# Gated retention: one matmul per four heads' exponents, with the split running sums flattened through HBM

## The reference, cut to what matters

```python
q = rmsnorm(x @ Wq); k = rmsnorm(x @ Wk); v = rmsnorm(x @ Wv)
g = x @ Wg
gt = jax.nn.log_sigmoid(x @ Wgt) / 16.0            # one log decay per token and head
...
bc = jnp.cumsum(g, axis=-1)                        # here g is gt, summed inside a chunk
decay = jnp.exp(bc[..., :, None] - bc[..., None, :])
A = jnp.einsum('bhnid,bhnjd->bhnij', q, k) * jnp.where(mask, decay, 0.0)
o_intra = jnp.einsum('bhnij,bhnjd->bhnid', A, v)
...                                                # plus what the chunks before hand on
o = rmsnorm(o)
o = jax.nn.silu(g) * o
return o @ Wo
```

## Time and profile before

| what | value |
|---|---|
| median of 3 runs | 2580.32 us (2579.85 to 2581.23) |
| profiled execution, its own time | 2581.53 us |
| its span, first to last instruction | 2579.4 us |
| busy share of the span | PE 91%, DVE 62%, ACT 43%, POOL 34% |
| mean granted TensorE clock | 0.963 |
| gated retention, first to last exponents of it | 1150.9 to 1998.7 us |

### The profile page before, as it was taken

How to read it: one execution, slowest core, us unless ns; L and a number is a source line. 1 busy time by engine, 2 the same in 40 slices (tenths; PEclk the granted TensorE clock), 3 DMA queues, 4 the chain that set the end, 5 groups by cost and what they waited for, 6 DMA issues and landing times. The chain is left out here.

```text
span 2579.4 us, 55940 instructions
## 1 busy us (share of the span) xinstructions
PE 2337.8 (91%) x20985; PEld 1606.7 (62%) x21080; DVE 1603.8 (62%) x3416; ACT 1102.1 (43%) x2397; POOL 875.9 (34%) x1231
## 2 busy tenths in 40 slices
PE   8988999999999997989999999999998799839996
PEld 6765666666666665556656666666665699726664
DVE  1227787777777776656666666666666499862222
ACT  2333333333333331236666666666665244402221
POOL 1111010111011110015566665666655355532342
PEclk9999999999999998989999999999999799859998
DMA  5100000000000000220000000000000022231330
GB/s 166 41 1 2 1 0 0 0 0 0 0 0 0 0 0 11 75 65 1 0 0 0 0 0 0 0 0 0 0 0 1 1 71 92 75 103 50 125 104 29
DMA packets 52744, 65.20 MB, mean 25 GB/s; under 512 B 5970, under 2 KB 45607, under 8 KB 52697
## 3 DMA queue, kind: packets, MB, share of 16 engines
q1 hardware_dynamic: 49624, 56.47, 6.8%
q0 software_dynamic: 3072, 8.07, 1.0%
HBM read 43.88 MB, written 20.97 MB: 25 GB/s over the span
## 5 line engine op out<-in xcount | busy, mean ns | idle before, releaser
L369 PE MATMUL B_ps_s<-B_xk,B_xT 128*32 128x308 f32 x4096 | 284.9, 424 | 12.8 <-ACT B_xk L504 12.8
L390 PE MATMUL B_ps_m<-B_wo,B_oT 128*128 128x256 f32 x1024 | 239.5, 387 | 2.1 <-ACT B_oT L523 2.1
L1513 DVE TENSOR_TENSOR D_att<-D_ps_s,D_dexp 128x1024 f32<-128x1024 f32 x128 | 154.5, 1207 | 131.9 <-ACT D_dexp L1331 122.4
L1083 POOL TENSOR_SCALAR_AFFINE_SELECT D_att<-D_att 128x1024 f32<-128x1024 f32 x128 | 139.9, 1093 | 259.7 <-DVE D_att L1513 259.7
L390 PEld LDWEIGHTS B_ps_m<-B_wo,B_oT 128*128 128x128 f32 x1024 | 190.5, 191 | 52.4 <-ACT B_oT L523 18.3
L491 ACT ACTIVATE B_prob<-B_prob 128x616 f32<-128x616 f32 x128 | 92.8, 725 | 300.3 <-DVE B_prob L602 300.3
L369 PEld LDWEIGHTS B_ps_s<-B_xk,B_xT 128*32 128x32 f32 x4096 | 124.4, 109 | 148.5 <-issue 26.1
L600 DVE TENSOR_REDUCE B_mx<-B_ps_s 128x8 f32<-128x616 f32 x128 | 101.1, 790 | 150.2 <-PE B_ps_s L369 150.2
L285 POOL TENSOR_TENSOR B_veps<-B_mv,eps 128x2 f32<-128x2 f32 x32 | 6.2, 194 | 537.3 <-DVE B_mv L584 537.3
L1091 POOL TENSOR_TENSOR D_orms<-D_oms,D_half 128x32 f32<-128x32 f32 x32 | 174.0, 5439 | 2.7
L1182 PE MATMUL D_ps_s<-D_q2T,D_kT 32*128 32x256 f32 x1024 | 146.7, 402 | 6.8 <-DVE D_att L1513 3.6
(11 more groups left out here) (297 smaller groups left out, 5155.5 us busy)
## 6 DMA issues: line engine op xcount, KB each, us to landing
res<-in_x SPq DMA_DIRECT2D x16, 512.0 KB, 3.3
x_d<-res SPq DMA_DIRECT2D x8, 1024.0 KB, 4.5
out<-E_fin SPq DMA_DIRECT2D x8, 1024.0 KB, 7.1
wi<-in_L_ffn_wi SPq DMA_DIRECT2D x8, 1024.0 KB, 4.9
wo<-in_L_ffn_wo SPq DMA_DIRECT2D x8, 1024.0 KB, 7.4
C_wgu<-in_L_ffn_gate_up SPq DMA_DIRECT2D x8, 512.0 KB, 3.5
C_wdn<-in_L_ffn_down_proj SPq DMA_DIRECT2D x8, 256.0 KB, 2.7
B_wqT<-in_L_xattn_WqT SPq DMA_DIRECT2D x1, 1024.0 KB, 11.8
```

The source lines that it names most:

```text
L369: last = nc.tensor.matmul(ps_s[u % 2][q * G:(q + 1) * G, g, 0:HQ * S], xT[:, par, k, (2 * u + g) * G:(2 * u + g + 1) * G], xk[:, par, k].r ...
L390: last = nc.tensor.matmul(ps_m[:, bank, 0:D], oT[:, m, t * P:(t + 1) * P], wo[:, m], start=m == 0, stop=m == MT - 1)
L1083: nc.gpsimd.affine_select(out=att[:, n % 2], in_=att[:, n % 2], compare_op=ALU.is_ge, fill=0.0, base=0, pattern=[[0, HT], [1, P]], channel ...
L1513: nc.vector.tensor_tensor(att[:, n % 2].rearrange("p h i -> p (h i)"), ps_s[:].rearrange("p a n -> p (a n)"), dexp[:, n % 2], ALU.mult).th ...
```

## The change

The four `sel` matmuls of a bank go away. One matmul per bank, with `F` stationary and 512 columns of a new tile `pick` moving, computes both terms. For that, rows 0 to 31 of `F` are ones, and rows 0 to 2 of `pick` hold the three parts of all heads' running sums of the batch, laid out in one row each. Getting 16 partitions of sums into one partition's row is done by DMA on SP's queue: the split sums now go to a tile `split`, from there to a scratch tensor `sums_d` in HBM and, separately, to `F`; a third transfer brings `sums_d` into `pick[0:3]`. PE waits for the last two (`flat_ready`).

To give the transfers time, DVE runs `split_sums(nb)` right after `attend(b, 2)` and ahead of `norm_apply(b + 2)`, and ACT runs `border_decay(nb)`, for which `split_sums` waits, ahead of the second `squares_v(nb)`. SP's `flatten_sums(0)` stands ahead of `prefetch`.

```diff
@@ retention_weights, load_retention_weights: sel and nsel (512 KB each) become pick (1 MB)
@@ gated_retention
+        split = sb("split", [P, NT, P], BF16)
+        sums_d = nc.dram_tensor("sums_d", (96, T), BF16, kind="Internal").ap()
...
         @block.sync
         def _(sp):
+            def flatten_sums(b, first=False):
+                sp.wait_ge(f_ready, b + 1)
+                sp.dma_start(sums_d, split[32:P].rearrange("p c i -> p (c i)")).then_inc(spilled, 16)
+                if not first:
+                    sp.wait_ge(e_done, b * U)
+                sp.dma_start(F[32:P], split[32:P]).then_inc(flat_ready, 16)
+                sp.wait_ge(spilled, b * 16 + 16)
+                sp.dma_start(pick[0:3], sums_d.rearrange("(s h) n -> s h n", s=3)[:, 0:H]).then_inc(flat_ready, 16)
+
+            sp.wait_ge(w_loaded, LOADED)
+            sp.wait_ge(set_ready, 1)
+            flatten_sums(0, first=True)
             prefetch(sp)
+            with sp.Fori(1, B) as b:
+                flatten_sums(b)
...
+            nc.gpsimd.memset(F[0:32], 1.0)
...
             def exponents(b, n):
                 c, r = n // 2, n % 2
+                heads = pick[:].rearrange("p (f g e) (c i) -> p c g f e i", f=2, e=2, c=NT)
                 for bank in range(2):
-                    pl = r * HT + bank * 4
-                    nc.tensor.matmul(ps_e[:, bank], F[:, c], nsel[:, pl:pl + 4], start=True, stop=False)
-                    for i in range(4):
-                        last = nc.tensor.matmul(ps_e[:, bank, i * P:(i + 1) * P], sel[:, pl + i], F[:, c], start=False, stop=i == 3)
+                    last = nc.tensor.matmul(ps_e[:, bank], F[:, c], heads[:, c, 2 * r + bank], start=True, stop=True)
                 last.then_inc(e_done, 1)
...
             def body(b, prev, nxt, nxt2):
                 nb = b + 1
-                pe.wait_ge(f_ready, b + 1)
+                pe.wait_ge(flat_ready, b * 32 + 32)
                 exponents(b, 0)
...
                     copy_vg(nb, 1)
+                    border_decay(nb)
                     squares_v(nb, 1)
-                    border_decay(nb)
...
-            def split_sums(b):
-                f, fr = F[:].rearrange("p c i -> p (c i)"), Fr[:].rearrange("p c i -> p (c i)")
+            def split_sums(b, first=False):
+                f, fr = split[:].rearrange("p c i -> p (c i)"), Fr[:].rearrange("p c i -> p (c i)")
                 dve.wait_ge(dec_ready, b + 1)
                 dve.wait_ge(bcT_done, b + 1)
+                if not first:
+                    dve.wait_ge(flat_ready, b * 32)
...
                 attend(b, 2)
+                if nxt:
+                    split_sums(nb)
                 if nxt2:
                     norm_apply(b + 2)
...
                 copy_state(b)
                 if nxt:
-                    dve.wait_ge(e_done, b * U + 4)
-                    split_sums(nb)
                     dve.wait_ge(av_done, b * U + 4)
                     scale_v(nb)
```

More of the change, by code:

```diff
@@ L903, in retention_positions @@
     return order
-RET_LOADS = 10
+RET_LOADS = 9
 def retention_weights(nc, ctx):
     shapes = {"wqk": [P, KD, 2 * D], "wvg": [P, KD, 2 * D], "wgt": [P, KD, RET_H], "wo": [P, KD, D], "upto": [P, P],
-              "after": [P, P], "head_mask": [P, 2], "block_mask": [P, P], "sel": [P, RET_H, P], "nsel": [P, RET_H, P]}
-    w = {k: ctx.enter_context(nc.sbuf_tensor("D_" + k, shape, BF16 if k in ("sel", "nsel") else F32)) for k, shape in shapes.items()}
+              "after": [P, P], "head_mask": [P, 2], "block_mask": [P, P], "pick": [P, RET_H, T]}
+    w = {k: ctx.enter_context(nc.sbuf_tensor("D_" + k, shape, BF16 if k == "pick" else F32)) for k, shape in shapes.items()}
     return w, ctx.enter_context(nc.semaphore("D_w_loaded"))
@@ L918, in load_retention_weights @@
         sp.dma_start(w[name][:], i["L1_attn_" + name].rearrange("(k p) n -> p k n", p=P)).then_inc(w_loaded, 16)
-    for name in ("upto", "after", "head_mask", "block_mask", "sel", "nsel"):
+    for name in ("upto", "after", "head_mask", "block_mask", "pick"):
         sp.dma_start(w[name][:], i[name]).then_inc(w_loaded, 16)
@@ L941, in psum @@
             return ctx.enter_context(nc.psum_tensor("D_" + name, shape, F32))
-        wqk, wvg, wgt, wo, upto, after, head_mask, block_mask, sel, nsel = (w[k] for k in (
+        wqk, wvg, wgt, wo, upto, after, head_mask, block_mask, pick = (w[k] for k in (
             "wqk", "wvg", "wgt", "wo",
@@ L948, in gated_retention @@
             "block_mask",
-            "sel",
-            "nsel"))
+            "pick"))
         st = sb("st", [P, NT, 6])
@@ L1019, in gated_retention @@
             sem, "z_step z_ready ld_ready f_step f_ready qk_ready v_ready att_raw state_ready oss_ready".split())
+        flat_ready, spilled = map(sem, "flat_ready spilled".split())
         y_step, y_ready, sg_step, sg_ready, res_ready = map(sem, "y_step y_ready sg_step sg_ready res_ready".split())
@@ L1031, in steps @@
             body(B - 1, prev=True, nxt=False, nxt2=False)
+        LOADED = 16 * RET_LOADS
         @block.sync
         def _(sp):
+            def flatten_sums(b, first=False):
[9 more added lines that the diff above has]
+            flatten_sums(0, first=True)
             prefetch(sp)
-        LOADED = 16 * RET_LOADS
+            with sp.Fori(1, B) as b:
+                flatten_sums(b)
         @block.gpsimd
@@ L1146, in running_sums @@
                 pe.wait_ge(ld_ready, b + 1)
-                nc.tensor.matmul(c_bc[:, 0:H], upto[:], ld[:, 1, 0, 0:H], start=True, stop=True)
-                nc.tensor.matmul(c_bc[:, H:2 * H], after[:], ld[:, 0, 0, 0:H], start=True, stop=True).then_inc(bc_done, 1)
+                nc.tensor.matmul(c_bc[:, 0:H], upto[:], ld[:, 1, 1, 0:H], start=True, stop=True)
+                nc.tensor.matmul(c_bc[:, H:2 * H], after[:], ld[:, 0, 1, 0:H], start=True, stop=True).then_inc(bc_done, 1)
                 for c in range(NT):
@@ L1493, in log_decay @@
                 dve.wait_ge(z_ready, b + 1)
-                for s in (0, 2, 3):
+                for s in (1, 2, 3):
                     last = nc.vector.tensor_tensor(ld[:, :, s, 0:H], zm[:], zl[:], ALU.subtract)
                 last.then_inc(ld_ready, 1)
-            def split_sums(b):
-                f, fr = F[:].rearrange("p c i -> p (c i)"), Fr[:].rearrange("p c i -> p (c i)")
+            def split_sums(b, first=False):
+                f, fr = split[:].rearrange("p c i -> p (c i)"), Fr[:].rearrange("p c i -> p (c i)")
                 dve.wait_ge(dec_ready, b + 1)
                 dve.wait_ge(bcT_done, b + 1)
+                if not first:
+                    dve.wait_ge(flat_ready, b * 32)
                 nc.vector.tensor_copy(f, c_bcT).then_inc(f_step, 1)
@@ L1592, in _ @@
             scale_qk(0)
-            split_sums(0)
+            split_sums(0, first=True)
             scale_v(0)
@@ L2526 @@
     arrays["block_mask"] = ((row // RET_D == col // RET_D) / 4).astype(np.float32)
-    heads = np.array([retention_head(p) for p in range(RET_H)])
-    of_head = (row % 32 == heads) & (row // 32 != 1)
-    arrays["sel"] = np.repeat(of_head[:, :, None], P, 2).astype(ml_dtypes.bfloat16)
-    arrays["nsel"] = -arrays["sel"]
+    of_head = (row % 32 == np.arange(RET_H)) & (row >= 32)
+    arrays["pick"] = -np.repeat(of_head[:, :, None], T, 2).astype(ml_dtypes.bfloat16)
     arrays = {k: np.ascontiguousarray(a) for k, a in arrays.items()}
```

## The result

The changed kernel takes 2733.72 us (median of 4 runs, 2729.45 to 2734.47), the kernel before 2580.78 us beside it: 1.058 times the time, with a 95% interval of 1.0571 to 1.0597. The forecast was 2737 us. The profiled execution's span is 2731.8 us.

A forecast was written before the change was run, and what follows sets the result against it. It took a 26.86 us loop of waits through DVE, POOL, PE and ACT as the bound. To 2581.53 us it added 0 for matmuls, 93 split, 5 first flattening and 57 clock: 2737 us, range 2672 to 2795.

The forecast's parts named there:

- What bounds the kernel: Whole batch: a loop of waits through DVE, POOL, PE and ACT closes after 26.86 us, without PE's exponents.
- Fewer matmuls: PE's exponents: 0.44 us freed four times a batch, 56 us of PE, all lost in waits; taken as 0.
- The split: DVE ahead of `norm_apply`: waiting for `dec` and splitting delay the state update 3.1 us in 30 batches, 93 us.
- The transfers: SP's queue after the split: 4 to 6 us in series under 10.6 us of cover; only batch 0 pays, 5 us.
- The clock: PE from state update to `transpose_qk`: the longer gap lowers the clock in every batch, 1.9 us each, 57 us.
- The sum: Whole kernel: 2581.53 us plus 0, 93, 5 and 57 gives 2736.5, say 2737 us.
- (a): PE's clock holds, so only split and first batch count: 2680 us; chance 0.14.
- (b): PE's lower clock lasts into the projections, costing 114 us: 2793 us; chance 0.12.
- (c): Transfers late, at 7 us each costing 3.4 us a batch more: 2839 us; chance 0.04.
- (d): PE paces the batch, the split is absorbed and the 56 us of matmuls come off: 2530 us; chance 0.04.

The follow-up runs named there:

- e2: Changed kernel with the old arithmetic on PE, each bank getting its four `sel` matmuls back: 2733.55 us.
- e9: Changed kernel with POOL's `keep_residual(b + 2)` moved behind `causal(b, 2)` and `qkv_scale(b + 1)`, DVE's queue untouched: 2597.66 us.
- e1: Changed kernel with DVE's split placed behind `norm_apply(b + 2)` in place of ahead of it: 2615.49 us.
- e5: Changed kernel with the split behind `norm_apply` and two extra unused matmuls a batch in PE's gap behind `values(b, 2)`: 2590.94 us.
- e3: Changed kernel with five extra unused matmuls a batch, one ahead of `values(b, 2)` and four behind it, in PE's gaps: 2682.40 us.
- e4: Changed kernel with the split back at its old place behind `copy_state`, so the transfers have no cover: 2710.64 us.
- e6: Kernel before, with DVE's `attend(b, 3)` and `add_out(b - 1)` ahead of `scale_qk(b + 1)`, and `gate_parts(b + 1)` ahead of `silu_inverse(b)`: 2571.63 us.
- e7: Changed kernel with split behind `norm_apply`, `attend(b, 3)` and `add_out(b - 1)` ahead of `scale_qk(b + 1)`, `gate_parts(b + 1)` ahead of `silu_inverse(b)`: 2535.92 us.

## Why the prediction was right, by its own steps

- **What bounds the kernel.** Right. "PE's exponents aren't in it": e2 brings the old ones back and the time stays, and e9 shows the link in POOL's queue that the waits of the earlier trace rows had pointed to.
- **Fewer matmuls, 0.** The size (0.44 us an `exponents`) is as predicted, and so is the zero in the changed kernel (e2). As a general price of this edit the zero may be too kind: in e1 the wait on PE is longer by about the freed time, and e5 shows that the lower clock behind this wait costs 25 us there. I had counted the freed time into the gap of the forecast, but not seen that it alone might be enough.
- **The split, 3.1 us a batch and 93 us.** Measured 4.30 - 1.14 = 3.16 us in the timelines, 30.15 - 27.08 = 3.07 us a steady batch, and 91 us between e3 and e5. Its parts: 1.38 us of wait for `dec` and 1.7 us of splitting.
- **The transfers, hidden; 5 us once.** Hidden in each steady batch. In series they take 3.75 us in e4 and 4.3 us in the first batch here (issued at 1150.20), at or a little below the low end of the 4 to 6 expected. The first `state` comes 7.8 us later, against 5. PE waits for the transfer once, and what follows runs at the lower clock (0.50 from 1155 to 1160 us, where it was 1.00):

```profile
1154.48 1.03 PE L1190 MATMUL D_ps_e<-D_pick,D_F 128*128 128x512 bf16 x2 [4.27 <-DMA D_pick<-sums_d]
```

The same wait is in e1, e3 and e5, and the first `state` is 3.1, 7.2 and 5.6 us late there. How much of these differences is the stage being reached at another time, no run parts.
- **The clock, 1.9 us a batch and 57 us.** Measured 51 us by e3: 31.55 - 29.93 = 1.62 us a batch on average, 31.86 - 30.15 = 1.71 us in a steady one. That is an average of three kinds of batch that take turns. In the one above, the clock is back at `values`, 1631.29 us, and the piece loses 1.25 us; the other two lose 1.76 and 2.31 us. The prediction had every batch lose the same four slowed steps.
- **The sum.** Predicted 155 us over the kernel before, measured 153: 91 for the split, 51 for the clock and 10 for first batch and remainder, against 93, 57 and 5. That the sum is right to 2 us is partly luck: the clock's term was 6 us too high and the last one 5 too low. The parts also hold only in this order of taking them away: with the split moved first (e1), 118 us come back at once and 25 are left for the clock.
- **The rivals.** (a) was made by hand in e3 and came out at 2682 us, its price of 2680; the clock doesn't hold by itself. (b) did not happen: the lower clock ends before the projections in every kind of batch. (c) would need nearly three times the measured duration of the transfers. (d) is wrong for this order of work, though by a narrow margin, and becomes true of e6, where it is PE that paces.

## What to carry to other kernels

A busy share of 93% doesn't make an engine the bound, though here it was only 0.35 us a batch from being it: follow the longest waits until they close, and price an edit by where its instructions stand in that loop. The same four instructions, with their wait for `dec`, cost 91 us in front of one neighbour and at most 10 behind it. And time saved on TensorE ahead of a wait may not be neutral: it goes into the gap, and in e1 a gap of 2.62 us cost 25 us by the lower clock, so shorten the loop first and save matmuls after.

## What the runs showed of the hardware

Adding work made the kernel faster twice, by 51 us (e3) and 25 us (e5). PE's gap of 1.23 us never let the clock fall in the steady batches. One of 2.40 to 2.45 us (e9) did in one batch of three, one of 2.62 us (e1) in three of six, and one of 4.17 us in all, behind another of 1.47 us (the changed kernel) as behind one of 0.29 us (e2). The length of the gap alone doesn't decide it, since equal gaps in e1 and e9 went both ways.

The same DVE instruction isn't always equally long. In e7 the second cast of the split has a median of 896 ns, and its first cast, alone, 0.42 us:

```profile
L1524 DVE CAST D_split<-D_Fr x32: 291/896/907, 1149.4 to 1931.6; 64x256 bf16<-64x256 f32 x32
```

Before, its median was 292 ns. In e7 it starts at 1528.42 us, while POOL's `causal(b, 2)` runs from 1528.08 to 1529.17 us; in the batch of the earlier trace rows POOL was not at work beside it. A shared way into SBUF would fit these numbers: the Trainium skill, "GPSIMD Engine Reference", section "Specifications", says that GpSimd shares its SBUF interfaces with VectorE, and that they contend with VectorE instructions in a two-port mode or with two SBUF inputs. No row shows in which mode the cast ran, and no run here parts this from other causes.
